# Layer 1's rounded softmax weights as bf16: a second GpSimd pass, bf16 transposes, a minimum in the take

## The chip, the cores and the metric

The kernel runs on one core of one Trainium2 chip. The metric is the device time of one execution in microseconds. In the profile TensorE is PE (its weight loads PEld), VectorE DVE, ScalarE ACT, GpSimd POOL and SyncE SP.

## What is computed

Four transformer layers work in turn on x (32 batches, 112 tokens, 256 channels), each with cross attention of 16 heads to the same context of 375 tokens; layers 1 and 3 have self attention too. Layer 1, the one that the change touches, quantises queries, keys, values and the softmax weights to 8 bits:

```python
def _fq(x, delta, zp, n_bits):
    xi = _round_ste(x / delta) + zp
    xq = jnp.clip(xi, 0.0, 2.0 ** n_bits - 1.0)
    return (xq - zp) * delta

sim = jnp.einsum('bhid,bhjd->bhij', _fq(q, dq, 128.0, 8), _fq(k, dk, 128.0, 8)) * SCALE
attn = jax.nn.softmax(sim, axis=-1)
out = jnp.einsum('bhij,bhjd->bhid', _fq(attn, dw, 0.0, 8), _fq(v, dv, 128.0, 8))
...
x = _attn(h1, h1, ...) + x          # self attention
x = _attn(h2, context, ...) + x     # cross attention
x = a * jax.nn.gelu(g, approximate=False) @ ff_w2 + ff_b2 + x
```

The weights become whole numbers from 0 to 255 (delta dw = 1/255).

## The kernel before

A stream is two batches, 224 tokens; there are 16 streams per layer. Attention works in units: one head of one batch in cross attention (scores of 112 by 375), four heads in self attention (112 by 448). Two units make a pair. A cross pair's way is: scores on TensorE into one of four PSUM banks; the maximum on VectorE (nmax, line 1411, and in layer 1 its scaling nmaxc, line 1415); the exponential with its sum on ScalarE (line 1305) into a slot of e (eight slots, so four pairs); the inverse of the sum on VectorE (rsum, line 1422, in layer 1 scaled to rsumw, line 1426); the weighing on GpSimd (line 1627 in layer 1, 1630 elsewhere) in place in e; three transposes on TensorE per cross unit (line 1152), four per self unit (line 1149), into one of four banks called ring; the take from the bank into probs (in layer 1 always on VectorE, line 1489); and the product with the values (lines 1190 and 1166 in layer 1), after all units of an octet are taken.

In layer 1 the weighing multiplies by rsumw and adds ROUND = 12582912, which rounds to a whole number in f32 and leaves it on the "shelf" of that constant. The take subtracts ROUND and limits to 255, and writes bf16. Layer 1's clipped queries, keys and values (lines 1460 to 1478) are bf16 too.

Each engine works through a list that is made before the kernel is built. `Plan` gives every step an engine, a cost and a place (`pos`); `list_steps` names the costs and `tensor_cost` those of TensorE's products; `arrange` then plays the engines forward and on each takes the ready step with the lowest place. So a cost moves no place, but it can move the order in which steps are taken, on every engine, and also which of VectorE and ScalarE takes a result that either may take. An exponential waits until the transposes of the pair four before are done (they free the slot of e); scores wait until the exponential of the pair two before is done. Any TensorE product waits until the bank of four products before is saved. The queues are in order: what stands behind a waiting step waits too.

Of the kernel before, what the change touches and what calls it, by code (L numbers as in the profile page):

```python
# [163 lines left out]
class Plan:  # L164
# [159 lines left out]

    def tensor_cost(self, j):
        if j.kind == "turn":
            return 0.35 if j.of.octet.attn == "cross" else 0.42
        if j.kind == "pv":
            if j.of.attn == "self":
                return 0.4 if j.layer == 1 else 0.9  # L330
            return (2.4, 0.45, 2.4, 1.3)[j.layer]
        if j.kind == "ck" or j.kind == "cvar":
            return mm(T, KC)
        if j.kind == "cv":
            return mm(512, KC) if j.layer == 2 else mm(D, 2 * KC) if j.m == 0 else mm(D, KC)
        if j.kind == "v":
            return mm(D, KC)
        if j.kind in ("o", "f2", "o2"):
            return mm(N, 8 if j.kind == "f2" else WEIGHTS[j.layer][j.kind][0])
        return mm(N, KC)  # L340
# [24 lines left out]
    def list_steps(self):  # L365
        for p in self.pairs:
            own, q = p.octet.attn == "self", p.octet.layer == 1
            scores = (0.3 if not own else 0.45) if q else (0.83 if not own else 1.2)
            self.add("scores", p, "T", scores, p.index)
            self.add("max", p, "V", (1.12 if own else 0.96) + (0.35 if q else 0), p.index + 0.3)  # L370
            self.add("exp", p, "A", 2.9 if own else 1.3, p.index + 0.5)
            self.add("invert", p, "V", 0.17 + (0.35 if q else 0), p.index + 0.9)
            self.add("weigh", p, "G", 2.7 if own else 1.15, p.index + 1.0)
        for j in self.jobs:
            self.add("job", j, "T", self.tensor_cost(j), j.pos)
            self.add("save", j, j.by, self.save_cost(j), j.pos + 0.2)
# [395 lines left out]
def four_layers(nc, x_in, ctx_in, w_in, v_in, c_in, causal_in, out):  # L772
    plan = Plan()
    with ExitStack() as stack:
# [80 lines left out]
        expd = sem("expd")  # L855
        inverted = sem("inverted")
        weighed = sem("weighed")
        zeroed = sem("zeroed")
        chain_v = sem("chain_v")

# [105 lines left out]
        def e_of(u):  # L966
            return e[0:S, slot(u), :]

        def probs_of(o, c, col, width):
            dt = BF16 if o.layer == 1 else F32  # L970
            if is_own(o):
                return part(probs[:, o.index % 2, :], 0, [16 * S], dt)[0:S, col * S:col * S + width]
            return part(probs[:, o.index % 2, :], 0, [CHUNKS, 8 * S], dt)[0:R, c, col * S:col * S + width]

        def take_parts(j):

            u, o = j.of, j.of.octet
            bank = ring[j.index % RING][:, :]
            if is_own(o):
                return probs_of(o, 0, 4 * u.k, 4 * S), bank[0:S, 0:4 * S]  # L980
            col = 4 * (u.k % 2) + u.k // 2 if o.layer in (0, 2) else u.k
# [67 lines left out]
                self.wait_ge(job_done, max([j.index for j in jobs], default=-1) + 1)  # L1049

        every, nth = plan.every, plan.nth

        def normed(wait, n):
            if n.layer == 0:
# [87 lines left out]

        def tensor_turn(pe, wait, j, ps):
            u, o = j.of, j.of.octet
            wait.wait_ge(weighed, nth["weigh", plan.pairs[u.index // 2]])
            dst, idt, src = ps[:, :], ident, e_of(u)
            if is_own(o):
                for n in range(4):
                    ins = pe.transpose(dst[0:S, n * S:(n + 1) * S], src[:, n * S:(n + 1) * S], idt[0:S, 0:S])  # L1149
            else:  # L1150
                for c in range(CHUNKS):
                    ins = pe.transpose(dst[0:R, c * S:(c + 1) * S], src[:, c * R:(c + 1) * R], idt[0:S, 0:S])  # L1152
# [328 lines left out]
        def vector_save(dve, wait, j):  # L1481
# [3 lines left out]
            if j.kind == "turn":  # L1485
                dst, src = take_parts(j)
                take_free(wait, j)
                if layer == 1:
                    ins = dve.tensor_scalar(dst, src, ROUND, 255.0, ALU.subtract, ALU.min)  # L1489
                else:  # L1490
                    ins = dve.tensor_copy(dst, src)  # L1491
            elif j.kind == "mean":
# [109 lines left out]
        def pool_program(pool):  # L1602
# [6 lines left out]
            for kind, x_ in plan.order["G"]:  # L1609
# [13 lines left out]
                for u in p.units:  # L1623
                    for n in range(count_of(o)):
# [4 lines left out]
                        else:  # L1629
                            ins = nc.gpsimd.tensor_scalar(mine, mine, rsum[0:S, slot(u), n:n + 1], 0.0,  # L1630
                                                          ALU.mult, ALU.add)
                ins.then_inc(weighed, 1)

# [133 lines left out]
```

## Time and profile before

| What | Value |
|---|---|
| Time, median of 3 runs | 5536.67 us (5536.1 to 5538.5) |
| The profiled execution | 5536.01 us, span 5534.2 us |
| Mean granted TensorE clock | 0.964 |
| TensorE busy | 5179.5 us (94%), weight loads 3763.0 us (68%) |
| VectorE busy | 3353.0 us (61%) |
| ScalarE busy | 2724.5 us (49%) |
| GpSimd busy | 1588.8 us (29%) |

The busy shares are means over four layers that differ. Layer 1 runs from about 980 to 2560 us, and 1112 to 2502 us is the stretch that is layer 1 alone. A granted clock of 1.00 is 2.4 GHz and 0.50 is 1.2 GHz. A wait counts in the stretch where it ends last; idle time of an engine that nothing waits for costs nothing.

### The profile page before, as it was taken

How to read it: one execution, taken by the hardware profiler on the slowest of the kernel's cores; microseconds unless marked ns; L12 is line 12 of the kernel's file. 1: busy time of each engine (PE TensorE's matmuls, PEld its weight loads, DVE VectorE, ACT ScalarE, POOL GpSimd, SP SyncE). 2: the span in 40 equal slices, each digit the busy share in tenths (PEclk: the TensorE clock that was granted, in tenths of full speed). 3: DMA queues.
4: the chain of work that ended last, by engine and by line, in shares of the span. 5: the costliest groups of instructions: out<-in, count | busy, mean ns of one | idle time of the engine just before them, and what ended most of it. 6: DMA issues, size and time to landing. Idle time of an engine off the chain costs nothing.

```text
span 5534.2 us, 90625 instructions
## 1 busy us (share of the span) xinstructions
PE 5179.5 (94%) x34496; PEld 3763.0 (68%) x34496; DVE 3353.0 (61%) x7775; ACT 2724.5 (49%) x8550; POOL 1588.8 (29%) x3090
## 2 busy tenths in 40 slices
PE   8999999877877778789999999999999999999999
PEld 5666666666666666666666666666667777777777
DVE  5555555777777777776544544544545666666665
ACT  4555555655555565554333223323334566556654
POOL 2333333433232332332111111111113333334332
PEclk9999999988989889889999999999999999999999
DMA  2000000100000000000100000000000100000000
GB/s 74 18 21 22 22 19 21 39 13 13 16 10 13 16 13 16 10 20 23 35 13 12 10 16 13 10 16 13 10 22 20 33 16 17 19 16 16 16 16 9
DMA packets 39744, 103.03 MB, mean 19 GB/s; under 512 B 4880, under 2 KB 21520, under 8 KB 38032
## 3 DMA queue, kind: packets, MB, share of 16 engines
q1 hardware_dynamic: 39312, 97.23, 5.7%
q8 instruction: 276, 4.52, 0.4%
q14 instruction: 156, 1.28, 0.1%
HBM read 82.53 MB, written 14.68 MB: 18 GB/s over the span
## 4 chain that ended last, share of the span: by engine, by line
PE 89%; ACT 6%; DVE 4%; issue 0%; DMA 0%; SPq 0%; ACTq 0%
PE ring L1201 51%; PE ring L1152 13%; PE score L1139 13%; ACT e L1305 4%; PE ring L1183 3%; PE ring L1176 3%; PE ring L1149 2%; PE ring L1190 2%; ACT work L1338 1%; PE ring L1166 1%; DVE nmax L1411 1%; DVE probs L1489 1%; DVE h L1438 1%; PE score L1134 0%; ACT heads L1288 0%
## 5 line engine op out<-in xcount | busy, mean ns | idle before, releaser
L1630 POOL TENSOR_SCALAR e<-e,rsum 112x375 f32<-112x375 f32 (+1 forms) x2048 | 1088.6, 547 | 2846.5 <-DVE rsum L1422 2845.8
L1411 DVE TENSOR_REDUCE nmax<-score 112x2 f32<-112x750 f32 (+1 forms) x1152 | 1098.1, 953 | 296.8 <-PE score L1139 295.9
L1305 ACT ACTIVATE e<-score,nmax 112x375 f32<-112x375 f32 (+1 forms) x2048 | 1043.1, 524 | 391.2 <-DVE nmax L1411 386.9
L1152 PEld LDWEIGHTS ring<-consts,e 112*125 112x125 f32 x6144 | 845.1, 195 | 339.4 <-issue 181.5
L1319 ACT COPY probs<-ring 125x336 f32<-125x336 f32 (+1 forms) x1009 | 415.6, 445 | 1318.8 <-PE ring L1152 1277.4
L1152 PE MATMUL ring<-consts,e 112*125 112x112 f32 x6144 | 961.1, 288 | 7.7 <-DVE values L1478 2.4
L1201 PE MATMUL ring<-h,weights 128*128 128x224 f32 x3840 | 901.1, 365 | 23.0 <-DVE values L1478 15.6
L1139 PE MATMUL score<-keys,q 64*112 64x375 f32 (+2 forms) x3584 | 771.3, 500 | 134.0 <-ACT e L1305 133.9
L1627 POOL TENSOR_SCALAR e<-e,rsumw 112x375 f32<-112x375 f32 (+1 forms) x1024 | 487.5, 493 | 1057.3 <-DVE rsumw L1426 1055.2
L1201 PEld LDWEIGHTS ring<-h,weights 128*128 128x128 f32 x3840 | 691.2, 194 | 126.2 <-issue 23.6
L1305 ACT ACTIVATE e<-score,nmaxc,quant 112x375 f32<-112x375 f32 (+1 forms) x1024 | 553.5, 562 | 221.1 <-PE ring L1149 110.9
L1201 PE MATMUL ring<-weights,ctx 128*125 128x256 f32 (+1 forms) x1536 | 557.6, 492 | 0.0
L1201 PE MATMUL ring<-ctx,weights 128*128 128x375 f32 x1536 | 556.6, 488 | 0.0
L1139 PEld LDWEIGHTS score<-keys,q 64*112 64x112 f32 (+2 forms) x3584 | 242.9, 164 | 444.7 <-issue 231.9
L1305 ACT ACTIVATION_READ_ACCUMULATOR e<-score,nmax 112x1 f32 x2048 | 430.9, 210 | 0.0
L1201 PE MATMUL ring<-heads,weights 128*128 128x224 f32 x1536 | 359.5, 380 | 58.3 <-DVE values L1478 57.0
L1201 PE MATMUL ring<-work,weights 128*128 128x224 f32 (+1 forms) x1792 | 399.7, 372 | 0.8 <-DVE work L1534 0.6
L1557 DVE COPY values<-ring 125x512 f32<-125x512 f32 (+2 forms) x444 | 209.5, 496 | 299.4 <-PE ring L1201 297.5
L1201 PEld LDWEIGHTS ring<-ctx,weights 128*128 128x128 f32 x1536 | 281.7, 192 | 144.1 <-issue 39.9
L1201 PEld LDWEIGHTS ring<-weights,ctx 128*125 128x125 f32 x1536 | 274.5, 187 | 150.9 <-issue 111.8
L1491 DVE COPY probs<-ring 125x336 f32<-125x336 f32 (+1 forms) x655 | 326.1, 514 | 55.2 <-PE ring L1152 48.7
L1201 PEld LDWEIGHTS ring<-heads,weights 128*128 128x128 f32 x1536 | 301.9, 204 | 82.5 <-DVE values L1478 60.1
(107 smaller groups left out, 5351.3 us busy)
## 6 DMA issues: line engine op xcount, KB each, us to landing
ctx<-ctx_t SPq DMA_DIRECT2D x128, 375.0 KB, 3.0
out_t<-x SPq DMA_DIRECT2D x64, 224.0 KB, 1.9
x<-out_t SPq DMA_DIRECT2D x48, 224.0 KB, 2.5
weights<-weights SPq DMA_DIRECT2D x5, 1024.0 KB, 5.0
x<-x_t SPq DMA_DIRECT2D x16, 224.0 KB, 2.5
weights<-weights SPq DMA_DIRECT2D x1, 3328.0 KB, 11.2
weights<-weights SPq DMA_DIRECT2D x1, 2560.0 KB, 9.0
weights<-weights SPq DMA_DIRECT2D x1, 2304.0 KB, 8.6
```

Of the source, the lines that this page charges most:

```text
L1139: ins = pe.matmul(score_bank(u)[0:S, n * width:(n + 1) * width], lhs, rhs, start=not masked, stop=not masked or n == nt - 1)
L1152: ins = pe.transpose(dst[0:R, c * S:(c + 1) * S], src[:, c * R:(c + 1) * R], idt[0:S, 0:S])
L1176: ins = pe.matmul(ps[64 * odd:64 * odd + 64, 0:4 * S], vs[0:R, c, kv:kv + 64], probs_of(o, c, 4 * odd, 4 * S), start=c == 0, stop=c == last)
L1183: ins = pe.matmul(ps[64 * odd:64 * odd + 64, i * S:(i + 1) * S], vs[0:R, c, hd:hd + 64], probs_of(o, c, 4 * odd + i, S), start=c == 0, sto ...
L1201: ins = pe.matmul(out_, a, b_, start=n == 0, stop=n == len(parts) - 1)
L1305: ins = nc.scalar.activation(e_of(u)[:, n * width:(n + 1) * width], score_bank(u)[0:S, n * width:(n + 1) * width], ACT.Exp, bias=minus, sc ...
L1319: ins = nc.scalar.copy(dst, src)
L1411: ins = dve.tensor_reduce(to, src, AX, ALU.max, negate=True)
L1491: ins = dve.tensor_copy(dst, src)
L1557: ins = dve.tensor_copy(dst, src)
L1627: ins = nc.gpsimd.tensor_scalar(mine, mine, rsumw[0:S, slot(u), n:n + 1], ROUND, ALU.mult, ALU.add)
L1630: ins = nc.gpsimd.tensor_scalar(mine, mine, rsum[0:S, slot(u), n:n + 1], 0.0, ALU.mult, ALU.add)
```

## The change

After the weighing of a layer-1 pair GpSimd waits for its own result and makes a second pass over each unit: times 1.0, plus -ROUND, from e in f32 into the first half of the same slot, read as bf16 (`steps_of`). One instruction covers a whole unit, 375 elements in cross and 448 in self attention. The transposes wait for the new semaphore `stepped`, use the bf16 identity `ident_b`, and write bf16 into the bank. The take reads bf16 from the bank and is a minimum with 255. The costs that the planner works with change too: less for the transposes of layer 1, more for its weighing.

```diff
--- before.py
+++ after.py
@@ -324,6 +324,8 @@
 
     def tensor_cost(self, j):
         if j.kind == "turn":
+            if j.layer == 1:
+                return 0.19 if j.of.octet.attn == "cross" else 0.25
             return 0.35 if j.of.octet.attn == "cross" else 0.42
         if j.kind == "pv":
             if j.of.attn == "self":
@@ -370,7 +372,7 @@
             self.add("max", p, "V", (1.12 if own else 0.96) + (0.35 if q else 0), p.index + 0.3)
             self.add("exp", p, "A", 2.9 if own else 1.3, p.index + 0.5)
             self.add("invert", p, "V", 0.17 + (0.35 if q else 0), p.index + 0.9)
-            self.add("weigh", p, "G", 2.7 if own else 1.15, p.index + 1.0)
+            self.add("weigh", p, "G", (2.7 if own else 1.15) + ((1.3 if own else 1.0) if q else 0), p.index + 1.0)
         for j in self.jobs:
             self.add("job", j, "T", self.tensor_cost(j), j.pos)
             self.add("save", j, j.by, self.save_cost(j), j.pos + 0.2)
@@ -855,6 +857,7 @@
         expd = sem("expd")
         inverted = sem("inverted")
         weighed = sem("weighed")
+        stepped = sem("stepped")
         zeroed = sem("zeroed")
         chain_v = sem("chain_v")
 
@@ -966,6 +969,10 @@
         def e_of(u):
             return e[0:S, slot(u), :]
 
+        def steps_of(u):
+
+            return e_of(u).bitcast(BF16)
+
         def probs_of(o, c, col, width):
             dt = BF16 if o.layer == 1 else F32
             if is_own(o):
@@ -976,6 +983,8 @@
 
             u, o = j.of, j.of.octet
             bank = ring[j.index % RING][:, :]
+            if o.layer == 1:
+                bank = bank.bitcast(BF16)
             if is_own(o):
                 return probs_of(o, 0, 4 * u.k, 4 * S), bank[0:S, 0:4 * S]
             col = 4 * (u.k % 2) + u.k // 2 if o.layer in (0, 2) else u.k
@@ -1049,6 +1058,14 @@
                 self.wait_ge(job_done, max([j.index for j in jobs], default=-1) + 1)
 
         every, nth = plan.every, plan.nth
+        eight_bit = {}
+        for kind, by in (("weigh", "G"),):
+            ps = [x_ for k_, x_ in plan.order[by] if k_ == kind and x_.octet.layer == 1]
+            eight_bit.update({(kind, p): i + 1 for i, p in enumerate(ps)})
+
+        def eight_bit_nth(p, kind):
+            return eight_bit[kind, p]
+
 
         def normed(wait, n):
             if n.layer == 0:
@@ -1142,8 +1159,14 @@
 
         def tensor_turn(pe, wait, j, ps):
             u, o = j.of, j.of.octet
-            wait.wait_ge(weighed, nth["weigh", plan.pairs[u.index // 2]])
+            p = plan.pairs[u.index // 2]
+            if o.layer == 1:
+                wait.wait_ge(stepped, eight_bit_nth(p, "weigh"))
+            else:
+                wait.wait_ge(weighed, nth["weigh", p])
             dst, idt, src = ps[:, :], ident, e_of(u)
+            if o.layer == 1:
+                dst, idt, src = dst.bitcast(BF16), ident_b, steps_of(u)
             if is_own(o):
                 for n in range(4):
                     ins = pe.transpose(dst[0:S, n * S:(n + 1) * S], src[:, n * S:(n + 1) * S], idt[0:S, 0:S])
@@ -1486,7 +1509,7 @@
                 dst, src = take_parts(j)
                 take_free(wait, j)
                 if layer == 1:
-                    ins = dve.tensor_scalar(dst, src, ROUND, 255.0, ALU.subtract, ALU.min)
+                    ins = dve.tensor_scalar(dst, src, 255.0, None, ALU.min)
                 else:
                     ins = dve.tensor_copy(dst, src)
             elif j.kind == "mean":
@@ -1630,6 +1653,13 @@
                             ins = nc.gpsimd.tensor_scalar(mine, mine, rsum[0:S, slot(u), n:n + 1], 0.0,
                                                           ALU.mult, ALU.add)
                 ins.then_inc(weighed, 1)
+                if o.layer == 1:
+                    wait.wait_ge(weighed, nth["weigh", p])
+                    full = count_of(o) * width
+                    for u in p.units:
+                        ins = nc.gpsimd.tensor_scalar(steps_of(u)[:, 0:full], e_of(u)[:, 0:full], 1.0, -ROUND,
+                                                      ALU.mult, ALU.add)
+                    ins.then_inc(stepped, 1)
```

GpSimd's list in layer 1, before (112x112 is a quarter of a self unit, 112x375 a cross unit; x24 are the weighings of twelve cross pairs):

```order
28 L1627 TENSOR_SCALAR e<-e,rsumw 112x375 x24
29 L1627 TENSOR_SCALAR e<-e,rsumw 112x112 x16
30 L1627 TENSOR_SCALAR e<-e,rsumw 112x375 x8
31 L1627 TENSOR_SCALAR e<-e,rsumw 112x112 x16
32 L1627 TENSOR_SCALAR e<-e,rsumw 112x375 x24
33 L1627 TENSOR_SCALAR e<-e,rsumw 112x112 x16
```

And after, some way into the layer:

```order
38 L1660 TENSOR_SCALAR e<-e 112x375 x2
39 L1650 TENSOR_SCALAR e<-e,rsumw 112x375 x2
40 L1660 TENSOR_SCALAR e<-e 112x375 x2
41 L1650 TENSOR_SCALAR e<-e,rsumw 112x112 x8
42 L1660 TENSOR_SCALAR e<-e 112x448 x2
43 L1650 TENSOR_SCALAR e<-e,rsumw 112x112 x8
44 L1660 TENSOR_SCALAR e<-e 112x448 x2
45 L1650 TENSOR_SCALAR e<-e,rsumw 112x375 x2
```

Behind each pair's weighing now stands a second pass of two instructions, with 448 elements each for self and 375 for cross units. The order of the pairs is the same.

TensorE's list where a stream's self attention begins (probs,values is the cross octet's product, probs,own the self octet's; score<-keys 112x112 the self scores), before:

```order
1261 L1201 MATMUL ring<-ctx,weights 128x375 x2
1262 L1139 MATMUL score<-keys,q 112x375 x6
1263 L1190 MATMUL ring<-probs,values 32x112 x24
1264 L1149 MATMUL ring<-consts,e 112x112 x8
1265 L1139 MATMUL score<-keys 112x112 x8
1266 L1149 MATMUL ring<-consts,e 112x112 x8
1267 L1201 MATMUL ring<-heads,weights 128x224 x2
1268 L1152 MATMUL ring<-consts,e 125x112 x3
1269 L1139 MATMUL score<-keys 112x112 x8
1270 L1152 MATMUL ring<-consts,e 125x112 x3
1271 L1166 MATMUL ring<-probs,own 32x112 x16
1272 L1201 MATMUL ring<-heads,weights 128x224 x2
```

And after:

```order
1252 L1156 MATMUL score<-keys,q 112x375 x2
1253 L1213 MATMUL ring<-probs,values 32x112 x24
1254 L1156 MATMUL score<-keys,q 112x375 x4
1255 L1172 MATMUL ring<-ident_b,e 112x112 x16
1256 L1224 MATMUL ring<-heads,weights 128x224 x2
1257 L1175 MATMUL ring<-ident_b,e 125x112 x3
1258 L1224 MATMUL ring<-heads,weights 128x224 x2
1259 L1189 MATMUL ring<-probs,own 32x112 x16
1260 L1175 MATMUL ring<-ident_b,e 125x112 x3
1261 L1156 MATMUL score<-keys 112x112 x8
1262 L1175 MATMUL ring<-ident_b,e 125x112 x3
1263 L1156 MATMUL score<-keys 112x112 x8
```

The sixteen self transposes stood in two groups of eight with a self score pair between; they now stand together, with two cross score pairs between them and the product in front, and the self score pairs behind them.

## Rows read from the trace of the kernel before

**Rows 1.** Of the page: the span in 40 slices, TensorE

```profile
PE   8999999877877778789999999999999999999999
```

**Rows 2.** Layer 1: length, PE, PEld, DVE, ACT, POOL busy, PEclk, DMA share, GB/s

```profile
1112.00:2502.00 1390.00, 1091.79 (x7386) 905.66 (x7385) 1040.41 (x2800) 801.78 (x2350) 430.66 (x900) 0.87 0.05 14
```

**Rows 3.** The chain of waits in that stretch, shares by line

```profile
by line: PE ring L1201 42.8%; ACT e L1305 13.0%; PE ring L1152 9.8%; PE ring L1149 5.5%; PE score L1139 3.7%; ACT work L1338 3.0%; PE ring L1190 2.3%; DVE h L1438 1.8%; ACT heads L1288 1.6%; DVE nmax L1411 1.6%; DVE probs L1489 1.4%; issue 
```

**Rows 4.** Pieces of that chain: start us, us, what

```profile
1628.86 1.69 PE ring L1149 x8
...
1640.24 1.87 PE ring L1152 x9
...
1702.11 0.64 PE ring L1152 x6
```

**Rows 5.** Groups by line and form, 1112 to 2502 us; busy us, mean ns, idle before

```profile
L1627 POOL TENSOR_SCALAR e<-e,rsumw 112x375 f32<-112x375 f32 x451 | 270.3, 612 | 832.9 <-DVE rsumw L1426 831.1
L1152 PE MATMUL ring<-consts,e 112*125 112x112 f32 x1356 | 233.9, 308 | 4.5 <-DVE values L1478 2.4 <-DVE h L1496 2.0
...
L1489 DVE TENSOR_SCALAR probs<-ring 125x336 bf16<-125x336 f32 x451 | 214.1, 499 | 22.0 <-PE ring L1152 18.4
...
L1627 POOL TENSOR_SCALAR e<-e,rsumw 112x112 f32<-112x112 f32 x448 | 159.1, 376 | 126.0 <-DVE rsumw L1426 126.0
L1201 PE MATMUL ring<-ctx,weights 128*128 128x375 f32 x228 | 91.8, 528 | 0.0
...
L1149 PE MATMUL ring<-consts,e 112*112 112x112 f32 x448 | 86.1, 363 | 0.0
...
L1139 PE MATMUL score<-keys,q 32*112 32x375 bf16 x452 | 82.0, 381 | 119.9 <-ACT e L1305 119.9
L1149 PEld LDWEIGHTS ring<-consts,e 112*112 112x112 f32 x448 | 70.0, 191 | 7.3 <-issue 4.9
L1489 DVE TENSOR_SCALAR probs<-ring 112x448 bf16<-112x448 f32 x112 | 68.0, 619 | 14.6 <-PE ring L1149 12.9
L1415 DVE TENSOR_SCALAR nmaxc<-nmax,quant 112x2 f32<-112x2 f32 x225 | 66.0, 294 | 8.0
...
L1474 DVE TENSOR_SCALAR keys<-work 128x375 bf16<-128x375 f32 x56 | 28.2, 503 | 1.9
...
L1460 DVE TENSOR_SCALAR work<-work 128x224 f32<-128x224 f32 x80 | 21.5, 269 | 24.3 <-ACT work L1338 24.3
L1139 PEld LDWEIGHTS score<-keys 32*112 32x112 bf16 x448 | 20.1, 160 | 50.8 <-ACT e L1305 47.0 <-issue 3.8
L1460 DVE TENSOR_SCALAR work<-work 128x375 f32<-128x375 f32 x56 | 19.3, 345 | 2.3 <-ACT work L1338 2.2
...
L1415 DVE TENSOR_SCALAR nmaxc<-nmax,quant 112x8 f32<-112x8 f32 x56 | 13.0, 232 | 2.0
```

**Rows 6.** Line 1627 in that stretch: durations ns, and its waiters

```profile
L1627 POOL TENSOR_SCALAR e<-e,rsumw x899: 351/585/1003, 1113.8 to 2501.6; 112x375 f32<-112x375 f32 x91, 112x112 f32<-112x112 f32 x89
...
who waited for it (us, times):
```

**Rows 7.** The same columns, two stretches of one stream

```profile
1621.59:1625.00 3.41, 0.73 (x4) 0.25 (x4) 1.95 (x6) 3.41 (x13) 1.70 (x6) 1.00 0.00 0
1625.00:1642.06 17.06, 12.95 (x98) 10.95 (x99) 12.22 (x28) 7.15 (x28) 4.55 (x9) 0.50 0.01 1
```

**Rows 8.** Instructions in order of time, 1624.5 to 1634 us

```profile
1624.30 4.21 POOL L1627 TENSOR_SCALAR e<-e,rsumw 112x112 f32<-112x112 f32 x9
...
1625.98 0.60 DVE L1415 TENSOR_SCALAR nmaxc<-nmax,quant 112x2 f32<-112x2 f32 x1
...
1628.79 1.74 PE L1149 MATMUL ring<-consts,e 112*112 112x112 f32 x8
```

**Rows 9.** Waits in layer 1: us, times, longest us

```profile
PE score L1139 <- ACT e L1305: 159.5, 108, 4.2
ACT e L1305 <- PE ring L1149: 99.2, 28, 4.8
```

## The prediction

> **What bounds the kernel now.** I read the busy shares first [rows 1], then the four layers as four stretches [rows 2], then the chain of waits inside layer 1, then the costs by line there. In layers 0, 2 and 3 TensorE's digits are nines, in slices 8 to 18 of 40 they are sevens and eights [rows 1]. That stretch is layer 1: TensorE is busy for 1091.79 of its 1390.00 us, its granted clock is 0.87 on average and VectorE is busy for 1040.41 us [rows 2]. So only in layer 1 do several engines share the bound, and only layer 1 is edited. In its chain [rows 3] TensorE's lines hold about two thirds: products 42.8%, the cross-attention transposes (L1152) 9.8%, the self-attention transposes (L1149) 5.5%, scores 3.7%. ScalarE's exponentials hold 13.0%, VectorE's take out of the transposes' bank (L1489) 1.4%. The pieces of one stream show how the transposes lie in it: 9 in 1.87 us, 6 in 0.64 us, 8 self ones in 1.69 us [rows 4]. The 6 in 0.64 us ran at 2.4 GHz (107 ns each), the 8 in 1.69 us at 1.2 GHz (211 ns each): in the stream from 1625 us the granted clock is 0.50 for 17.06 us, after a stretch with TensorE busy for only 0.73 of 3.41 us [rows 7].
>
> **The transposes.** Of each layer-1 transpose the data, the identity and the result become bf16; the number of instructions stays 2048 (512 cross units by 3, 128 self units by 4). The trace has no full-array bf16 transpose. The nearest pair of rows moves 375 columns with both types: the bf16 scores take 82.0 us for 452, 0.181 us each, the f32 products from ctx 91.8 us for 228, 0.403 us each: 0.45 of the time [rows 5]. The bf16 scores use 32 rows of the array and neighbours may overlap, so 0.45 is the good end. The bad end is no gain, if loading the weights sets the pace. Against that end: 448 bf16 weight loads of 112 columns keep the loader busy for 20.1 us, the same number in f32 for 70.0 us [rows 5]. I take one half. On the chain the two lines hold 15.3% of 1390 us = 213 us, for 1804 transposes; scaled to all 2048 (the rest lie where layer 1 overlaps its neighbours) 241 us. Half of it is **-120 us**, the ends 0 and -133.
>
> **The take.** VectorE's take reads bf16 from PSUM, and the subtraction is gone, which costs nothing today since both operations are in one instruction. It takes 499 ns for 336 elements and 619 for 448 [rows 5], 1.07 ns per element. The bad end is the same 499 ns. The good end is the pace at which one-input operations of this engine run from SBUF: 269 ns for 224 and 345 for 375 elements [rows 5], 0.50 ns per element, which gives 499 - 336 x 0.57 = 307 ns. I take the good end, because nothing but the element size is in the way: 512 x 0.19 + 128 x 0.26 = 131 us of VectorE's time, of which the chain holds 1.4% of 1390 = 19 us (22 for the whole layer), times 0.38: **-8 us**, the ends 0 and -8.
> The Trainium skill (VectorE: DVE Perf Modes, section "Why PSUM operands drop a tier") lets a PSUM operand run at two elements per cycle if it is 2 bytes wide and at one if it is f32; the f32 half agrees with the 1.07 ns here, the other half no row of this kernel shows.
>
> **The second GpSimd pass.** Per cross pair two more instructions of 375 elements, per self pair two of 448. The first pass costs 270.3/451 = 0.60 us for 375 and 159.1/448 = 0.355 us for 112 [rows 5], so 0.93 ns per element and 0.67 us for 448. Added: 512 x 0.60 + 128 x 0.67 = 393 us of GpSimd, which is busy for 430.66 of 1390 us now [rows 2]; it goes to about 56% of that stretch. GpSimd is no bound. The ends for the new instruction are 0.355 us, its fixed part, and 1.0 us, the longest of the first pass [rows 6].
> The latency is what counts: a pair's transposes wait for 1.2 us more (1.33 self), plus the wait of the second pass for the first. Nobody waits for the first pass in layer 1: the list of its waiters is empty, and 899 instructions stand there [rows 6]. At a place that recurs in every stream, the self pair at 1624.30, GpSimd's nine instructions run until 1628.51 and the ninth is already the next pair's; eight at 0.355 us end near 1627.1, and the transposes start at 1628.79 [rows 8]. There 1.33 us just fits. And the order shown above now has two score pairs between the heads' product and the self transposes. Cost on the path **0**; if the cover is gone, see the first rival.
> What is queued behind: the next pair's first pass. ScalarE then waits for a slot of e, which is free only when the pair four back has been transposed; it waits so for 99.2 us now, for self transposes [rows 9]. This wait partly shrinks with faster transposes, so I add nothing.
>
> **The shared way into SBUF.** A two-element scaling by VectorE (nmaxc, L1415) averages 232 ns in the form with 8 elements and 294 in the form with 2 [rows 5], so it isn't size. At 1625.98 it takes 0.60 us while GpSimd's 4.21 us run is under way [rows 8]: it waits for the GpSimd instruction to end. Today that excess is 225 x 62 ns = 14 us for nmaxc, and for the clip's operations (L1474 averages 503 ns for 375 elements where L1460 needs 345, 56 times) 9 us [rows 5]; with the other operations of this kind I estimate 30 us in all. GpSimd's share goes from 31 to 56%, so about 30 x 0.8 = 24 us more on VectorE, less than the 131 it saves. These operations stand between scores, exponentials and weights, often on the chain; I charge **+10 us**, the ends 0 and +40.
> The Trainium skill (SBUF — State Buffer, section "SBUF: two separate sides") says the same in stronger words: the pair of ports is an exclusive lock for the whole instruction. The 0.60 us agrees; it speaks against this change.
>
> **Sum.** -120 - 8 = -128 us come off the chain as it stands. Not all of it stays: in these in-order queues the next late thing is near. TensorE already waits 159.5 us in layer 1 for exponentials [rows 9], and shorter transposes lengthen such waits; the ring of four banks comes free at VectorE's pace. I keep 0.6 of it, since VectorE, the second most loaded engine, gets relief too: -77. With +10: **-67 us**. The profiled execution took 5536.01 us (span 5534.2 and 1.8 outside it), the median shown is 5536.67: 5469 us. The terms' ends: keeping all and no contention, -133 - 8 = 5395; keeping nothing and +10 to +40, 5546 to 5576.
>
> **Rivals.**
> 1. *Transposes become late and hold the exponentials* (slower). Place: the self pairs, where the margin is thinnest [rows 8] and ScalarE's 99.2 us for L1149 arise [rows 9]. For it: an exponential needs the slot of four pairs back, and the order now lets more scores go ahead of the self transposes. Against: no wait for GpSimd at all today. Price: 64 self pairs by 1.33 us = 85 us. -67 + 85 = +18: 5554 us. It decides once a self pair loses over 1.05 us.
> 2. *The clock*. TensorE has less to do while its waits for ScalarE stay, and low stretches follow such waits [rows 7]. Time X more at 1.2 GHz costs X/2 of TensorE's work, times its two thirds of the chain: X/3. 200 us more (mean clock 0.80 in place of 0.87) eat the whole gain: 5536 us; half of that leaves 5503. For it: the 17.06 us stretch holds 12.95 us of TensorE work, transposes among it. Against: the same work becomes shorter, also at 1.2 GHz, where it gains double.
> 3. *The types bring nothing*: weight loading paces the transposes and the take stays at 499 ns. Then only the pass remains: +10: 5546 us. Against: the loader rows above.
> 4. *All of it stays* and the schedule closes up: 5395 to 5410 us.
>
> **Chances.** Forecast (5410 to 5520) 0.69; rival 4 0.06; rival 2 in its weak form (faster still) 0.05 and in its full form 0.06; rival 1 0.08; rival 3 0.06. Faster by over 0.2% (11 us, about what can be told from no change here) 0.79, within it 0.07, slower 0.14. Range for 8 in 10: 5408 to 5542.
>
> **What would show it.** The transposes' lines at half their busy time (320 us for 1804 now); the take near 310 ns; GpSimd near 56% in layer 1 with still no TensorE wait on it; nmaxc's mean above 294 ns; the mean clock in layer 1 at 0.85 or more; stretches of layers 0, 2 and 3 unchanged in length. Wrong would be a take at 499 ns, an exponential's wait for L1149's successor above 100 us, or a clock near 0.80.

## The result, and the profile after

The changed kernel takes 5557.3 us (median of 6, 5553.53 to 5560.91), the kernel before 5536.39 us beside it: a ratio of 1.0038, 95% interval 1.0025 to 1.0051. The change makes it slower by 21 us. I had forecast 5469 us with 5408 to 5542 for 8 in 10, and gave slower 0.14. The profiled execution spans 5551.7 us.

The page after: the span, the busy times, and TensorE's share and granted clock in the 40 slices.

```profile
span 5551.7 us, 91354 instructions
...
PE 5119.0 (92%) x34496; PEld 3679.8 (66%) x34496; DVE 3282.4 (59%) x7791; ACT 2722.3 (49%) x8534; POOL 1929.5 (35%) x3730
...
PE   8999999877767777779999999999999999999999
...
PEclk9999999877888888889999999999999999999999
```

Against [rows 1] TensorE's digits sink by one in slices 11, 12, 16 and 18, and nowhere else. VectorE's total fell by 70.6 us from 3353.0, GpSimd's rose by 340.7 us. TensorE's busy time fell by 60.5 us, its idle time (span less busy) rose from 354.7 to 432.7 us. The mean clock sank from 0.964 to 0.952. Since the clock has two levels, twice the missing share times the span is the time at 1.2 GHz: by the clock's records inside the span 399 us before and 536 us after.

The stretch of layer 1, with the columns of [rows 2]:

```profile
1112.00:2502.00 1390.00, 1025.11 (x7330) 822.22 (x7328) 970.24 (x2790) 791.82 (x2320) 719.90 (x1453) 0.83 0.05 14
```

The chain there, shares by line (L1224 are the products, L1175 and L1172 the transposes, L1328 the exponentials):

```profile
by line: PE ring L1224 46.5%; ACT e L1328 16.6%; PE ring L1175 4.8%; PE score L1156 4.4%; DVE nmax L1434 3.8%; ACT work L1361 3.3%; PE ring L1172 3.0%; issue 1.9%; ACT heads L1311 1.6%; DVE work L1483 1.4%; DVE rsumw L1449 1.4%; PE ring L12
```

The transposes' share of the chain fell from 15.3% to 7.8% as forecast [rows 3], and what took their place are products (42.8 to 46.5%), exponentials (13.0 to 16.6%) and the maximum (1.6 to 3.8%).

The forms that answer to [rows 5]: busy us, mean ns, idle time before.

```profile
L1660 POOL TENSOR_SCALAR e<-e 112x375 bf16<-112x375 f32 x446 | 227.9, 528 | 19.5
...
L1175 PE MATMUL ring<-ident_b,e 112*125 112x112 bf16 x1344 | 144.8, 239 | 3.6 <-DVE values L1501 2.0 <-DVE keys L1497 1.6
L1512 DVE TENSOR_SCALAR probs<-ring 125x336 bf16<-125x336 bf16 x446 | 135.4, 324 | 29.9 <-PE ring L1175 28.7
...
L1449 DVE TENSOR_SCALAR rsumw<-rsum,quant 112x2 f32<-112x2 f32 x223 | 65.5, 294 | 7.9
L1438 DVE TENSOR_SCALAR nmaxc<-nmax,quant 112x2 f32<-112x2 f32 x223 | 65.3, 293 | 7.9
...
L1660 POOL TENSOR_SCALAR e<-e 112x448 bf16<-112x448 f32 x112 | 61.7, 567 | 4.9
...
L1172 PE MATMUL ring<-ident_b,e 112*112 112x112 bf16 x448 | 48.8, 278 | 31.4 <-DVE keys L1497 31.4
...
L1512 DVE TENSOR_SCALAR probs<-ring 112x448 bf16<-112x448 bf16 x112 | 41.6, 389 | 30.6 <-PE ring L1172 30.6
...
L1449 DVE TENSOR_SCALAR rsumw<-rsum,quant 112x8 f32<-112x8 f32 x56 | 22.6, 403 | 2.0
```

The scaling of rsumw before, for the last two:

```profile
L1426 DVE TENSOR_SCALAR rsumw<-rsum,quant 112x2 f32<-112x2 f32 x226 | 54.7, 242 | 8.0
...
L1426 DVE TENSOR_SCALAR rsumw<-rsum,quant 112x8 f32<-112x8 f32 x56 | 12.9, 231 | 2.0
```

Busy time by count, the transposes take 0.108 and 0.109 us each where they took 0.172 and 0.192. That is 0.61 of the time for both together, where I had taken one half. The take needs 324 and 389 ns where it needed 499 and 619; the good end of my bound was 307. The second pass takes 528 ns for 375 elements and 567 for 448, less than my 600 and 670. But rsumw's scaling went from 242 to 294 ns for two elements and from 231 to 403 for eight, which is no matter of size.

Who waits for the second pass (the list is empty again, as in [rows 6]), and the waits that answer to [rows 9]:

```profile
L1660 POOL TENSOR_SCALAR e<-e x558: 517/522/748, 1115.3 to 2501.8; 112x375 bf16<-112x375 f32 x148, 112x448 bf16<-112x448 f32 x38
...
who waited for it (us, times):
```

```profile
PE score L1156 <- ACT e L1328: 251.1, 113, 3.9
...
ACT e L1328 <- PE ring L1172: 66.7, 29, 6.4
```

TensorE's scores wait 251.1 us for exponentials, 92 us more than before. The exponentials' wait for self transposes went from 99.2 to 66.7 us, so my first rival (transposes late, +1.33 us per self pair) did not come in.

One self stage in order of time, to set beside [rows 8]:

```profile
1628.78 2.97 POOL L1650 TENSOR_SCALAR e<-e,rsumw 112x112 f32<-112x112 f32 x8 [4.85 <-DVE rsumw L1449]
...
1631.84 1.10 POOL L1660 TENSOR_SCALAR e<-e 112x448 bf16<-112x448 f32 x2
1631.86 0.57 DVE L1449 TENSOR_SCALAR rsumw<-rsum,quant 112x8 f32<-112x8 f32 x1
...
1635.73 1.10 POOL L1660 TENSOR_SCALAR e<-e 112x448 bf16<-112x448 f32 x2
...
1637.23 0.63 DVE L1497 TENSOR_SCALAR keys<-work 128x375 bf16<-128x375 f32 x1
...
1637.92 1.74 PE L1172 MATMUL ring<-ident_b,e 112*112 112x112 bf16 x16 [2.22 <-DVE keys L1497]
...
1639.02 0.66 ACT L1328 ACTIVATE e<-score,nmaxc,quant 112x375 f32<-112x375 f32 x1 [3.93 <-PE ring L1172]
```

GpSimd's second pass begins at 1631.84, and rsumw's scaling, from 1631.86, needs 0.57 us where its mean before was 0.23. The self transposes start only at 1637.92, 16 together, which are those of two pairs. The second pass of the first pair ended 5 us earlier, at 1632.94, that of the second pair 1.1 us earlier, at 1636.83. What ends last before them is VectorE's writing of the keys (until 1637.86), which frees a bank: not the pass, but here with only 1.1 us to spare.

### The profile page after: what moved, and what is told of

Same layout as the page of the kernel before. It is cut to its first block, busy times and chain, and to the rows that moved or that the text cites. A ratio compares the mean times of both kernels' runs of the same rounds, so it can differ in the third digit from the quotient of the medians.

```text
span 5551.7 us, 91354 instructions
## 1 busy us (share of the span) xinstructions
PE 5119.0 (92%) x34496; PEld 3679.8 (66%) x34496; DVE 3282.4 (59%) x7791; ACT 2722.3 (49%) x8534; POOL 1929.5 (35%) x3730
## 4 chain that ended last, share of the span: by engine, by line
PE 88%; ACT 7%; DVE 4%; issue 1%; DMA 0%; SPq 0%; ACTq 0%
PE ring L1224 52%; PE score L1156 14%; PE ring L1175 12%; ACT e L1328 5%; PE ring L1199 3%; PE ring L1206 3%; PE ring L1213 2%; PE ring L1172 2%; DVE nmax L1434 1%; ACT work L1361 1%; PE ring L1189 1%; PE score L1151 0%; ACT heads L1311 0%; DVE work L1483 0%; DVE rsumw L1449 0%
## 5 line engine op out<-in xcount | busy, mean ns | idle before, releaser
L1328 ACT ACTIVATE e<-score,nmax 112x375 f32<-112x375 f32 (+1 forms) x2048 | 1044.7, 525 | 385.5 <-DVE nmax L1434 381.2
L1156 PE MATMUL score<-keys,q 64*112 64x375 f32 (+2 forms) x3584 | 790.1, 508 | 243.9 <-ACT e L1328 243.9
L1224 PE MATMUL ring<-h,weights 128*128 128x224 f32 x3840 | 938.9, 378 | 76.1 <-DVE keys L1494 59.8
L1224 PEld LDWEIGHTS ring<-h,weights 128*128 128x128 f32 x3840 | 718.9, 200 | 187.8 <-DVE keys L1494 65.4
L1175 PEld LDWEIGHTS ring<-consts,e 112*125 112x125 f32 x4608 | 600.0, 188 | 303.0 <-issue 172.3
L1175 PE MATMUL ring<-consts,e 112*125 112x112 f32 x4608 | 697.1, 282 | 2.4 <-DVE q L1490 2.2
L1328 ACT ACTIVATE e<-score,nmaxc,quant 112x375 f32<-112x375 f32 (+1 forms) x1024 | 554.1, 568 | 190.3 <-DVE nmaxc L1438 108.9
L1224 PE MATMUL ring<-weights,ctx 128*125 128x256 f32 (+1 forms) x1536 | 575.5, 505 | 5.6 <-DVE own L1501 5.6
L1224 PE MATMUL ring<-ctx,weights 128*128 128x375 f32 x1536 | 555.7, 488 | 0.4 <-DVE values L1501 0.2
L1328 ACT ACTIVATION_READ_ACCUMULATOR e<-score,nmax 112x1 f32 x2048 | 430.3, 210 | 0.0
L1224 PE MATMUL ring<-work,weights 128*128 128x224 f32 (+1 forms) x1792 | 400.3, 372 | 1.7 <-DVE q L1490 1.0
L1224 PEld LDWEIGHTS ring<-weights,ctx 128*125 128x125 f32 x1536 | 281.9, 193 | 159.9 <-issue 111.8
L1224 PEld LDWEIGHTS ring<-ctx,weights 128*128 128x128 f32 x1536 | 285.8, 194 | 149.0 <-issue 41.7
L1224 PE MATMUL ring<-heads,weights 128*128 128x224 f32 x1536 | 357.2, 379 | 1.7 <-DVE keys L1494 1.3
L1224 PEld LDWEIGHTS ring<-work,weights 128*128 128x128 f32 x1792 | 330.8, 190 | 30.1 <-DVE q L1490 1.4
```

Source lines behind the costliest of these rows:

```text
L1156: ins = pe.matmul(score_bank(u)[0:S, n * width:(n + 1) * width], lhs, rhs, start=not masked, stop=not masked or n == nt - 1)
L1224: ins = pe.matmul(out_, a, b_, start=n == 0, stop=n == len(parts) - 1)
L1328: ins = nc.scalar.activation(e_of(u)[:, n * width:(n + 1) * width], score_bank(u)[0:S, n * width:(n + 1) * width], ACT.Exp, bias=minus, sc ...
```

## The experiments

All times are medians with the ratio to the kernel before, run beside them. Three theories: A, the planner's new costs made a worse order; B, the second pass holds VectorE or the exponentials; C, TensorE, with less to do, spends more time at 1.2 GHz and loses there what it saved.

**e1: the order of before.** The two cost edits are taken back, all else stays:

```diff
-            if j.layer == 1:
-                return 0.19 if j.of.octet.attn == "cross" else 0.25
...
-            self.add("weigh", p, "G", (2.7 if own else 1.15) + ((1.3 if own else 1.0) if q else 0), p.index + 1.0)
+            self.add("weigh", p, "G", 2.7 if own else 1.15, p.index + 1.0)
```

> The changed kernel with the planner's costs of before, so with the order of before on every engine, and the second pass, the bf16 transposes and the short take kept. Theory A (the new costs made a worse order, the work itself gains): 5470 to 5510 us, under the 5536 of before. Theory B (the second pass holds exponentials or VectorE in any order): 5550 us or more. Theory C (less TensorE work in layer 1 sends the clock down and that eats the gain in any order): 5530 to 5560 us, with the mean clock of layer 1's stretch near 0.83 as in the changed kernel.

Measured 5569.09 us, 1.0062 (1.0049 to 1.0075), mean clock 0.946. Without the new order the changed kernel is 12 us slower still, so the new order alone is not what made the change slow.

**e2: the order alone.** The kernel before with only the two cost edits (the diff's first two hunks).

> The kernel before with the planner's new costs alone: f32 transposes, one GpSimd pass, the take with its subtraction, in the changed order. Theory A: clearly slower than 5536, by 40 to 90 us, since the same order with all the savings is at 5557. Theories B and C: within 15 us of before.

Measured 5611.48 us, 1.0138 (1.0124 to 1.0152). The same order costs 76 us on the work of before and gains 12 us on the new work. An order has no price of its own.

**e5: no second pass.** As e1, and transposes wait for the first pass; what they read is then the f32 weights' bits taken as bf16, so this kernel leaves out the taking off of the shelf, and its layer-1 weights are not the reference's (nor are those of e8 and e12):

```diff
-                wait.wait_ge(stepped, eight_bit_nth(p, "weigh"))
+                wait.wait_ge(weighed, nth["weigh", p])
...
-                if o.layer == 1:
-                    wait.wait_ge(weighed, nth["weigh", p])
...
-                    ins.then_inc(stepped, 1)
```

> As e1 (order of before, bf16 transposes and take), and the second GpSimd pass is left out: the transposes read the slots of e as they are, so layer 1's weights are not the reference's. Theory B: at least 40 us under e1. Theories A and C: within 10 us of e1; the contention that goes is worth my 10 us.

Measured 5515.86 us, 0.9964 (0.9951 to 0.9978). Theory B's 40 us are there: in this order the second pass costs 53 us. And all the savings together, in the order of before and without the pass, are worth 20 us, not 128.

**e7: the pass alone,** on the kernel before:

```diff
...
+                    for u in p.units:
+                        ins = nc.gpsimd.tensor_scalar(e_of(u)[:, 0:full], e_of(u)[:, 0:full], 1.0, 0.0,
+                                                      ALU.mult, ALU.add)
                 ins.then_inc(weighed, 1)
```

> The kernel before, with f32 transposes and its own order, and a second GpSimd pass over each layer-1 unit (times 1, plus 0, f32 in place) for which the transposes wait: the pass's latency and contention without any of the savings. Theory B: 5600 us or more. Theories A and C: 5540 to 5560 us (my +10 for the contention, and little for the wait).

Measured 5590.19 us, 1.01 (1.0086 to 1.0114): +55 us, between the numbers that I had written for B and for A and C, and the same price as in e1 less e5.

**e12: the pass aside.** Is it the wait of the transposes or GpSimd's load? As e5, with a pass for which nobody waits:

```diff
...
+                    fixed = mean_w[0:S, 0:n_].unsqueeze(1).to_broadcast([S, c_, n_])
+                    for i in range(2):
+                        wait.wait_ge(stepped, passes[0])
...
+                        nc.gpsimd.tensor_scalar(spare_b[0:S, 0:c_ * n_].rearrange("p (c n) -> p c n", c=c_), fixed,
+                                                1.0, -ROUND, ALU.mult, ALU.add).then_inc(stepped, 1)
```

> As e5 (order of before, transposes right behind the first pass, layer 1's weights not the reference's), and GpSimd does a second pass of the same size per unit, from a constant tile into a spare bf16 tile, for which no transpose waits. So GpSimd's time and its hold on the way into SBUF are as in e1 (5569), and the transposes' wait for the second pass is gone. If the 53 us between e5 and e1 are the contention and the longer queue on GpSimd: 5555 to 5570 us. If they are the wait of the transposes for the second pass: 5516 to 5530 us. My prediction had 10 us for the contention and nothing for the wait.

Measured 5565.89 us, 1.0054 (1.0041 to 1.0067). 50 of the 53 us come back with the load alone; the wait for the pass is worth 3 us. A longer queue on GpSimd does not show as the way by which the load acts: between 1000 and 2600 us TensorE waits 0.4 us for GpSimd in e12, 0.2 in e5 and 11.5 in e1, and no wait of VectorE or ScalarE is put down to it. Two forms of VectorE in layer 1 without the pass (e5), and then with it aside (e12); they read and write SBUF and have no tie to the pass but that they run beside it:

```profile
L1499 DVE TENSOR_SCALAR values<-work 125x128 bf16<-125x128 f32 x174 | 33.7, 249 | 2.0
...
L1481 DVE TENSOR_SCALAR work<-work 128x224 f32<-128x224 f32 x80 | 22.2, 278 | 33.7 <-ACT work L1359 33.7
```

```profile
L1500 DVE TENSOR_SCALAR values<-work 125x128 bf16<-125x128 f32 x168 | 43.3, 315 | 1.9
...
L1482 DVE TENSOR_SCALAR work<-work 128x224 f32<-128x224 f32 x78 | 31.6, 406 | 30.3 <-ACT work L1360 29.5
```

Values go from 249 to 315 ns, the clip of 224 columns from 278 to 406. Not every operation pays: the takes, which read PSUM, stay at 328 and 329 ns (125x336), the maximum at 932 and 931, and the clip of 375 columns at 350 and 349. VectorE's busy time over the whole span rises from e5's 3243.1 (below) to 3294.0 us:

```profile
PE 5152.6 (93%) x34496; PEld 3698.2 (66%) x34496; DVE 3294.0 (59%) x7775; ACT 2725.6 (49%) x8550; POOL 1932.5 (35%) x3730
```

That is 51 us more for the same work, and the kernel is 50 us slower. e1 against e5 has 44 us and 53 us, e7 against the kernel before 54 us and 55 us. I had 24 us on VectorE and 10 on the path. All three pairs are in the order of before; two more follow below.

**e8: each layer-1 transpose twice,** as e5 otherwise:

```diff
-                for c in range(CHUNKS):
+                for c in (0, 1, 2) * (2 if o.layer == 1 else 1):
```

(and the same for the four of a self unit).

> As e5 (order of before, no second pass, bf16 transposes and take), and TensorE does each layer-1 transpose twice, so that its work there is about that of the f32 transposes again. Layer 1's weights are not the reference's. Theory C (TensorE's shorter work sends its clock down and that eats the gain): the time at 1.2 GHz falls from 506 us towards the 399 of before, and the time is within 10 us of e5's 5516 or under it although TensorE does more. Theory A/B (the transposes' time counts on the chain as I summed it, the clock follows by chance): 5516 plus 60 to 120 us.

Measured 5540.75 us, 1.0004 (0.9995 to 1.0013). e5 and e8, span and busy times:

```profile
span 5515.0 us, 90625 instructions
...
PE 5126.4 (93%) x34496; PEld 3681.0 (67%) x34496; DVE 3243.1 (59%) x7775; ACT 2722.0 (49%) x8550; POOL 1584.8 (29%) x3090
```

```profile
span 5541.1 us, 94721 instructions
...
PE 5201.0 (94%) x36544; PEld 3780.8 (68%) x36544; DVE 3254.3 (59%) x7775; ACT 2726.3 (49%) x8550; POOL 1586.7 (29%) x3090
```

TensorE does 108 us more work, counted at full clock, and the kernel is 25 us slower (22 by the two ratios): neither of the two expectations, nearer to C. The account is this. TensorE's span is busy time plus idle time. Its busy time inside the low stretches, added up from the trace's records, is 314.0 us before, 395.6 in e5, 329.0 in e8 and 386.5 in the changed kernel; half of each is what the low clock cost, if all that TensorE does takes twice as long there. So:

| | work at full clock | idle | lost to 1.2 GHz | span |
|---|---|---|---|---|
| before | 5022.5 | 354.7 | 157.0 | 5534.2 |
| e5 | 4928.6 | 388.5 | 197.8 | 5515.0 |
| e8 | 5036.5 | 340.1 | 164.5 | 5541.1 |
| e1 | 4923.0 | 409.2 | 235.1 | 5567.2 |
| changed | 4925.8 | 432.7 | 193.3 | 5551.7 |

The first column bears out the halving: over all traces it comes to 5021.9 to 5022.5 us in the four kernels with the work of before, and to 4923.0 to 4934.1 in the eleven with the short transposes once each, whatever their order and clock. From before to e5, 94 us of work go; 34 come back as idle time and 41 at the lower clock. From e5 to e1 TensorE's own work stays the same, and 21 us of idle time and 37 at the lower clock are added. e8 also bears on the take's worth: it has TensorE's work of before (14 us more), the short take with 99 us less on VectorE (3353.0 to 3254.3), and the time of before. In this order the short take bought at most what those 14 us hide.

**e9, e10, e11, e13: fillers.** To hold the clock, TensorE issues useless bf16 matmuls where its trace shows idle time of over 0.9 us: in e9 (the changed kernel), e10 (e1) and e11 (the kernel before) ahead of any step, after a wait for the next product's bank; in e13 (e1) in a product's own bank alone, whose edit this is:

```diff
+                for _ in range(WARM.get(j.index, 0)):
+                    pe.matmul(ps[:, 0:64], ident_b[:, :], ident_b[:, 0:64], start=True, stop=True)
```

> The changed kernel, and at 117 places of TensorE's list in layer 1 where its trace shows over 0.9 us of idle time, TensorE issues about as many useless bf16 matmuls of 64 columns (4620 in all) into the bank that its next product will use. Theory C: the time at 1.2 GHz falls from 537 us to under 300 and the kernel comes to 5480 to 5530 us. If the clock doesn't matter: 5557 or more, by what the fillers delay.

> The same fillers (139 places, 3966) in e1, the changed kernel in the order of before. Theory C: from 5569 to 5480 to 5530 us, time at 1.2 GHz from 602 us to under 300. Otherwise 5569 or more.

> The same fillers (126 places, 3496) in the kernel before. It has 399 us at 1.2 GHz. Theory C: 5490 to 5520 us; it gains less than e9 and e10, having less low time to win back. Otherwise 5536 or more.

> As e1 (5569 us, 602 us at 1.2 GHz), with fillers as in e10 but at 67 places only (3468 of them), where TensorE is about to start a product that waits for something else, in that product's own bank once it is free; so no wait is added. If the clock is what ate the gain: time at 1.2 GHz under 450 us and 5520 to 5550 us. If the clock only follows from the waits: within 10 us of 5569 or above.

Measured 5641.89, 5633.43, 5613.13 and 5618.12 us: 49 to 85 us slower than the kernel that each was put into. They lowered the time at 1.2 GHz to 502 us in e9 (from 536), 502 in e10 (from 601) and 478 in e13 (from 601), and left it in e11 (406, from 399). By the account above e13 has 105 us more work than e1, 54 us less lost to the low clock and 3 us less idle time. The row of e13's fillers shows why they don't answer the question:

```profile
L1142 PE MATMUL ring<-ident_b 128*128 128x64 bf16 x3420 | 154.1, 218 | 158.3 <-DVE values L1512 86.4 <-DVE h L1530 36.0 <-DVE keys L1508 19.4
```

Of the stretch they take 154.1 us, and 158.3 us of waiting stand ahead of them, 86.4 of it for VectorE's clipping of values. The idle time was the wait for the bank itself, so the fillers ran after it and not in its place. What the clock would bring if held at no cost was not measured.

**e14, e15: one pass in place of two.** GpSimd writes e times rsumw plus 1024 as fp16, whose step is 1 there, so that the write itself rounds:

```diff
-                            ins = nc.gpsimd.tensor_scalar(mine, mine, rsumw[0:S, slot(u), n:n + 1], ROUND,
+                            at = steps_of(u)[:, 2 * n * width:2 * n * width + width]
+                            ins = nc.gpsimd.tensor_scalar(at, mine, rsumw[0:S, slot(u), n:n + 1], SHELF,
                                                           ALU.mult, ALU.add)
...
-                    ins = dve.tensor_scalar(dst, src, 255.0, None, ALU.min)
+                    ins = dve.tensor_scalar(dst, src, SHELF, 255.0, ALU.subtract, ALU.min)
```

e14 has the order of before, e15 the new cost of the transposes.

> One pass in place of two: GpSimd writes e times rsumw plus 1024 as fp16, whose step there is 1, so the write rounds to a whole number; transposes in fp16, the take subtracts 1024 and limits to 255, from fp16. Order of before. It has e5's savings without the second pass: 5510 to 5525 us, if fp16 goes at the pace of bf16 on all three engines. If GpSimd's write to fp16 is slower or the take with two operations loses the faster pace: 5535 us or more.

> As e14, with the planner's new cost for layer 1's transposes (0.19 and 0.25 in place of 0.35 and 0.42) and the weighing's cost of before. If the bad order of e2 (+76 us on the kernel before) comes from the weighing's higher cost: at or under e14. If it comes from the transposes' lower cost: 20 to 70 us over e14.

e14: 5516.71 us, 0.9968 (0.9956 to 0.9981), e5's time with the whole computation. e15: 5534.87 us, 0.9999 (0.9990 to 1.0008), 18 us more by one cost.

**e3, e4: one cost each** in the changed kernel.

> The changed kernel (two passes) with the planner's cost of before for layer 1's transposes, and its new, higher cost for the weighing. The full change is at 5557 us, with both costs old (e1) 5569. If the weighing's new cost is what makes the order fit the second pass: 5545 to 5560 us. If it makes a bad order and the transposes' cost repairs it: over 5575 us.

> The changed kernel with the new cost for the transposes alone. e15 has the same order with one pass, and is 18 us over e14, which has the order of before. If orders add up: 5569 + 18 = 5587 us. If not, the order's worth hangs on the second pass.

e3: 5569.56 us, 1.0060 (1.0048 to 1.0073); e4: 5542.13 us, 1.0009 (1.0001 to 1.0018). The transposes' new cost gains 27 us here (e1 to e4) and loses 18 us with one pass (e14 to e15). My sum of 5587 for e4 was 45 us off.

**e16, e17, e18, e19: a third cost,** of layer 1's take, which the change shortens and whose cost it leaves at 0.5:

```diff
         if j.kind == "turn":
-            return 0.5
+            return 0.34 if j.layer == 1 else 0.5
```

> As e14 (5517 us), with the planner told that layer 1's take costs 0.34 in place of 0.5, which is nearer to the 329 and 385 ns measured. If orders move the time at random by 10 to 20 us: anywhere from 5500 to 5540. If truer costs make better orders: 5505 to 5515.

> The kernel before with the planner's cost of layer 1's take at 0.34 in place of 0.5 and nothing else changed; its take still needs 499 and 619 ns. e16 gained 94 us over e14 by this number with the short take. If the gain is the shorter take, which counts once the order leaves VectorE less slack around it: 5530 us or slower. If that order is better for any kernel: 5440 to 5500 us.

> As e1 (5569 us: two passes, bf16 transposes, short take, transposes' and weighing's costs of before) with the take's cost at 0.34. If the order's gain of 94 us carries over and the second pass keeps its price of 53 us: 5475 us, give or take 15. If orders and passes don't add: anywhere from 5460 to 5570.

> The changed kernel as it is (5557 us, both new costs) with the take's cost at 0.34 besides, so that all three costs that the change alters are told to the planner. If the missing third cost is what spoilt the change: 5460 to 5500 us. If not: 5540 us or more.

| | the take's cost at 0.5 | at 0.34 |
|---|---|---|
| work of before | 5536 | e17: 5454.94, 0.9856 (0.9839 to 0.9872) |
| two passes, bf16 | e1: 5569 | e18: 5436.37, 0.9822 (0.9807 to 0.9836) |
| one pass, fp16 | e14: 5517 | e16: 5422.75, 0.9795 (0.9781 to 0.9808) |
| two passes, new costs | the change: 5557 | e19: 5491.07, 0.9920 (0.9905 to 0.9935) |

The number 0.34 is wrong for the kernel before, whose take needs 499 ns, and e17 gains 81 us by it all the same. So the cost of 0.34 gives a better order to each of the four kernels, my "5530 or slower" for e17 was wrong, and truer costs are not why. e16 and e17, span and busy times:

```profile
span 5423.9 us, 90665 instructions
...
PE 5112.9 (94%) x34496; PEld 3670.3 (68%) x34496; DVE 3243.9 (60%) x7780; ACT 2722.2 (50%) x8546; POOL 1596.8 (29%) x3090
```

```profile
span 5445.0 us, 90664 instructions
...
PE 5163.7 (95%) x34496; PEld 3743.6 (69%) x34496; DVE 3339.6 (61%) x7779; ACT 2723.6 (50%) x8546; POOL 1585.3 (29%) x3090
```

TensorE's idle time is 311.0 us in e16 (e14: 387.0) and 281.3 in e17 (before: 354.7), the mean clock 0.958 (e14: 0.954) and 0.969 (before: 0.964). In e16, from 1112 to 2390 us, the weighing to fp16 (112x375) and the take read:

```profile
L1654 POOL TENSOR_SCALAR e<-e,rsumw 112x375 f16<-112x375 f32 x449 | 269.8, 601 | 700.3 <-DVE rsumw L1451 679.9
...
L1514 DVE TENSOR_SCALAR probs<-ring 125x336 bf16<-125x336 f16 x448 | 132.4, 326 | 2.7 <-PE ring L1177 2.3
```

601 ns for the pass that was 612 in f32 [rows 5]: rounding on the write costs GpSimd nothing.

**What the second pass costs in each order.** e14 takes e5's time, so a kernel with the one fp16 pass can stand for one without the second pass, and the runs hold four such pairs:

| order | without | with the second pass | time | VectorE busy |
|---|---|---|---|---|
| of before, work of before | before | e7 | +55 | +54 |
| of before | e5 | e1 | +53 | +44 |
| transposes' new cost | e15 | e4 | +7 | +19 (3252.8 to 3271.9) |
| take's cost | e16 | e18 | +14 | +37 (3243.9 to 3281.0) |

The same 330 to 343 us more on GpSimd cost 55 us in one order and 7 in another. The changed kernel's own order, with both new costs, is in none of the pairs.

## Why the prediction was wrong

1. *Where the bound lies, and that only layer 1 moves*: right; the slices outside it are unchanged.
2. *The transposes, -120 us on the chain*: their speed was a little off (0.61 of the busy time in place of one half; the chain's share halved, and 94 us of work at full clock are gone). The step from the chain's share to time was wrong.
3. *The take, -8 us*: speed right, its worth in the order of before about nothing.
4. *The second pass, wait 0, contention +10 us*: the wait was nearly right (3 us). The contention is mis-sized in the order of before: 44 to 54 us of VectorE's time in place of 24, and +50 to +55 on the path in place of 10. I scaled only the forms whose excess I had seen; in e1 and e12 the clip of 224 columns and the values, at their clean 269 and 255 ns before, joined them. In the two other orders the pass costs 7 and 14 us, which my 10 meets by luck, since I had not thought of the order. In the changed kernel the clip rose to 344 ns and the values stayed at 244. An estimate for its own order: e2 has 3369.0 us on VectorE in it, the short takes save 110 (before to e5) to 119 us (by their means), and the changed kernel has 3282.4, so 23 to 32 us are the pass's.
5. *"I keep 0.6 of it"*: the step that failed. e5 kept 20 of 128 us, 0.16, and under the take's cost the change of types kept 32 (e17 to e16), 0.25. Of e5's 94 us of work 34 turned into waits and 41 went to 1.2 GHz. My second rival had that mechanism, priced at a third of the low time; from before to the changed kernel the low time did rise, by 136 us. But 78 us of idle time came with it, which that rival had not counted.
6. *The order*: I read it for two waits and gave it no price. It is worth -12 us in the changed kernel and +76 in the kernel before; one more cost, of the take, is worth -81 in the kernel before and -133 in e1, which is more than the whole saving of 128 that I summed.

Of my signs, the take (324 ns), GpSimd's share (719.90 of 1390 us, 52%) with no wait of TensorE on it, and the exponentials' 66.7 us came out as written. The transposes at 0.61, the scaling of nmaxc at 293 ns and not above 294, and the clock at 0.83, under 0.85, did not.

Added up in the order of before, the parts are -20 (savings), +53 (second pass) and then -12 (new order): 5536 + 21 = 5557. In that order it is the second pass's load on GpSimd that makes the same work slower than before, shown by e12. Added up another way, by e15 and e4, the parts are -1 (savings with the transposes' new cost), +7 (second pass) and +15 (the weighing's new cost, e4 to the change). Both sums are true, so how much of the 21 us is the pass's depends on the order in which it is asked, and in the changed kernel's own order no run took the pass away. What both ways have in common is that the savings bring 20 us or less and not 77. With the take's cost at 0.34 the same work gains (5436 us in e18 against 5455 in e17). What stays open is why that order is better, and how much of the idle time and how much of the clock each causes the other.

e16 is faster than both kernels, by 113 us against before.

## What to carry to other kernels

Where several engines in order share a bound, the chain's share of a line is no estimate of what its saving brings: here a sixth of it came through in one order and a quarter in another. Before a saving is judged, run the old work in the new order and the new work in the old; an order that one planner cost moves can be worth more than the edit. Work put on an idle GpSimd can be paid for by VectorE's operations in SBUF, also by those with clean durations before, and whether that reaches the path hangs on the order (7 to 55 us here).

## What the runs showed of the hardware

- 330 to 348 us more of GpSimd work added 44 to 54 us to VectorE's busy time with unchanged operations in the order of before, 19 and 37 us in two others. VectorE's takes and maximum, which read PSUM, kept their durations. The Trainium skill (SBUF — State Buffer, section "SBUF: two separate sides") calls the pair of ports an exclusive lock held for the whole instruction; the 0.57 us of an operation whose mean was 0.23 before agrees.
- VectorE takes 336 bf16 or fp16 elements out of PSUM in 324 to 329 ns and 448 in 380 to 389, where f32 needed 499 and 619. The 112 elements more cost 52 to 65 ns, in f32 120. This is the faster pace that the Trainium skill (VectorE: DVE Perf Modes, section "Why PSUM operands drop a tier") allows 2-byte operands.
- TensorE's layer-1 transposes done twice (e8) brought the time at 1.2 GHz from 505 down to 413 us.
- GpSimd's write to fp16 rounds to the whole numbers that are needed (e14 and e16 give the reference's output) and costs no more than f32 (601 against 612 ns).
